# Extra unread matmuls in TensorE's waits, and another order of GpSimd's extra work, in a decoder layer on one core

## The reference

```python
x = layernorm(x + attention(x))              # 16 heads of 16, causal, softmax
x = layernorm(x + mamba(ctx, gate=x))        # state space block, see below
x = layernorm(x + moe(x))                    # 8 experts, the 2 best of each token
```

```python
state = state * exp(delta_t * A[n]) + (delta_t * u_t) * B_t[n]
y_t  += state * C_t[n]
y = (y + D * u) * silu(x)
```

## Time and profile before

| | us |
|---|---|
| median of 3 runs | 428.63 (428.04 to 429.7) |
| the profiled execution, its own time | 431.48 |
| its span in the trace | 429.7 |
| TensorE matmuls, busy | 340.4 (79%) |
| VectorE, busy | 252.1 (59%) |
| ScalarE, busy | 209.9 (49%) |
| GpSimd, busy | 248.5 (58%) |
| mean granted clock of TensorE | 0.878 |

### The profile page before, as it was taken

The page is one execution under the profiler, slowest core; times in us unless marked ns, Lnnn a source line. Parts: engine busy times, 40 slices in busy tenths (PEclk is TensorE's granted clock), DMA queues, the critical chain, the costliest instruction groups (busy, mean ns, idle before and its releaser), DMA issues.

```text
span 429.7 us, 5678 instructions
## 1 busy us (share of the span) xinstructions
PE 340.4 (79%) x1780; PEld 205.5 (48%) x1780; DVE 252.1 (59%) x439; ACT 209.9 (49%) x488; POOL 248.5 (58%) x232
## 2 busy tenths in 40 slices
PE   8794868856778677875869586899999999999651
PEld 4352435623446244653435242466666666666441
DVE  2989797974958879688977676112122222222134
ACT  4678786737877678767964100322222222212103
POOL 2075999999978996789888302233233333331214
PEclk9986596965989769896986888999999999999967
DMA  7050110162114510242106950111111111111162
GB/s 209 8 101 3 38 35 31 47 219 50 50 50 82 188 50 26 65 148 84 51 24 218 374 193 0 49 41 46 37 51 49 50 49 37 50 37 38 37 195 99
DMA packets 29455, 34.46 MB, mean 80 GB/s; under 512 B 4074, under 2 KB 23826, under 8 KB 29426
## 3 DMA queue, kind: packets, MB, share of 16 engines
q1 hardware_dynamic: 24770, 26.36, 20.3%
q0 software_dynamic: 2208, 6.03, 4.6%
q10 hardware_dynamic: 2448, 1.71, 1.4%
HBM read 28.92 MB, written 5.18 MB: 79 GB/s over the span
## 4 chain that ended last, share of the span: by engine, by line
PE 36%; DVE 6%; DMA 2%; ACT 2%; POOL 2%; issue 2%; DVEq 0%; POOLq 0%; ACTq 0%
PE psS L1600 18%; PE psD L1619 5%; PE psO L1619 4%; PE psD L1610 2%; PE psS L1450 2%; PE psT L1595 1%; DMA c_rows<-z_out 1%; DVE experts L981 1%; POOL rstd L493 1%; DVE u_sb L1131 1%; PE psT L1379 1%; DMA delta<-x_rows,row_in 1%; DMA z_out<-delta,row_out 1%; PE psT L1444 0%; POOL rstd L492 0%
## 5 line engine op out<-in xcount | busy, mean ns | idle before, releaser
L1600 PE MATMUL psS<-experts,delta 128*128 x184 | 86.5, 593 | 0.5 <-ACT delta L818 0.5
L504 POOL TENSOR_TENSOR experts<-experts,c_rows 128x1024 f32<-128x1024 f32 x31 | 73.0, 2355 | 17.8 <-DVE experts L981 17.4
L981 DVE TENSOR_TENSOR_SCAN experts<-experts,psD 128x512 f32<-128x512 f32 x64 | 74.4, 1204 | 0.0
L572 POOL DMA_INDIRECT z_out<-delta,row_out x23 | 22.8, 991 | 88.4 <-ACT delta L832 88.4
L1379 PE MATMUL psT<-ident,probs_at 128*128 128x128 f32 x192 | 39.2, 340 | 23.4 <-ACT probT L727 23.4
L1205 DVE COPY u_sb<-psD 128x512 f32<-128x512 f32 x23 | 15.9, 692 | 68.7 <-PE psD L1610 68.7
L689 ACT ACTIVATE experts<-delta,A_sb 128x255 f32<-128x255 f32 x128 | 54.7, 517 | 0.5 <-DVE du L929 0.5
L972 DVE TENSOR_TENSOR psD<-du,psD 128x512 f32<-128x512 f32 x64 | 41.6, 688 | 13.2 <-PE psD L1337 12.9
L1600 PEld LDWEIGHTS psS<-experts,delta 128*128 128x128 f32 x184 | 33.1, 190 | 24.3 <-issue 23.3
L1379 PEld LDWEIGHTS psT<-ident,probs_at 128*128 128x128 f32 x192 | 27.4, 172 | 35.1 <-ACT probT L727 33.4
L507 POOL TENSOR_TENSOR experts<-experts 128x512 f32<-128x512 f32 x31 | 40.7, 1312 | 2.4
(11 more groups left out here) (236 smaller groups left out, 591.6 us busy)
## 6 DMA issues: line engine op xcount, KB each, us to landing
c_rows<-c_dram SPq DMA_DIRECT2D x32, 256.0 KB, 3.4
experts<-in_L_ffn_w_gate_dram SPq DMA_DIRECT2D x8, 512.0 KB, 5.9
experts<-in_L_ffn_w_up_dram SPq DMA_DIRECT2D x8, 512.0 KB, 6.9
experts<-in_L_ffn_w_down_dram SPq DMA_DIRECT2D x8, 512.0 KB, 8.1
x_in<-in_x_dram SPq DMA_DIRECT2D x4, 256.0 KB, 5.3
x_rows<-x_sb SPq DMA_DIRECT2D x4, 256.0 KB, 2.5
probs_at<-z_out SPq DMA_DIRECT2D x4, 256.0 KB, 5.1
c_rows<-z_out ACTq DMA_DIRECT2D x4, 256.0 KB, 6.3
```

The source lines that it names most:

```text
L504: pool.tensor_tensor(states[:, g % ST], states[:, g % ST], c_rows[:, g % CR].rearrange("p n (o s) -> p n o s", o=1).broadcast_to([P, 2, HA ...
L981: dve.tensor_tensor_scan(states[:, g % ST, n].rearrange("p h s -> p (h s)"), dA[:, g % DA, n].rearrange("p h s -> p (h s)"), psD[:, n, :], ...
L1600: ins = pe.matmul(psS[:, bank, :], xgT[:, s % 2, k, :], gate_up_of(bass.ds(e, 1), i)[:, k, :], start=(k == 0), stop=(k == FC - 1))
```

## The change

GpSimd does both splits and all four fixes before its first product. The inverse deviation of batch b moves from ahead of the first product of batch b + 1 into the last product of batch b, behind its first instruction (for the last batch, whose last product is VectorE's, it stays). `keep_warm` takes a bank. TensorE gets unread matmuls: fourteen at step 0 of the first batch and eight at step 0 of the later ones (into `psT`), two, one and four at step 4 of each batch, two more there in the last one, and twenty-four in front of the combination. Two waits for `prob_rdy` that an earlier wait of the same engine includes are left out.

```diff
@@ -478,9 +478,10 @@
 
             pool.wait_ge(zeroed, 1 + DA)
             pool.wait_ge(ones_rdy, 1)
-            split_bc(0)
-            fix_log(0)
-            fix_log(1)
+            for th in range(TH):
+                split_bc(th)
+            for b in range(B):
+                fix_log(b)
 
             def inverse_deviation(k, n, done, count):
 
@@ -504,10 +505,12 @@
                 pool.tensor_tensor(states[:, g % ST], states[:, g % ST], c_rows[:, g % CR].rearrange(
                     "p n (o s) -> p n o s", o=1).broadcast_to([P, 2, HALVES, S]), ALU.mult).then_inc(hC_rdy, 1)
                 pool.wait_ge(hC_rdy, g + 1)
+                b, m = divmod(g, NP)
+                if m == NP - 1:
+                    inverse_deviation(2 * b, 0, x1_rdy, b)
                 pool.tensor_tensor(states[:, g % ST, 0], states[:, g % ST, 0], states[:, g % ST, 1],
                                    ALU.add).then_inc(pair_rdy, 1)
                 pool.wait_ge(pair_rdy, g + 1)
-                b, m = divmod(g, NP)
                 if m == 0:
                     pool.wait_ge(skip_rdy, HALVES * (b + 1))
                 else:
@@ -522,15 +525,8 @@
             link(pool.memset(exponent[:], -0.5))
             for b in range(B):
                 for m in range(NP):
-                    if m == 0 and b > 0:
-                        inverse_deviation(2 * (b - 1), 0, x1_rdy, b - 1)
                     if NP * b + m < STEPS - 1:
                         multiply_c(NP * b + m)
-                    if b == 0 and m < 2:
-                        fix_log(2 + m)
-                    elif b == 0 and m == 4:
-                        pool.wait_ge(y_sum, 5)
-                        split_bc(1)
                     if m == 1 and b > 0:
                         gate_output(b - 1)
                     if m == 3 and b > 0:
@@ -1445,9 +1441,9 @@
                                         start=(k == 0), stop=(k == FC - 1))
                 ins.then_inc(logit_ps, 1)
 
-            def keep_warm(n):
+            def keep_warm(n, bank=psS[:, 3, :]):
                 for _ in range(n):
-                    pe.matmul(psS[:, 3, :].rearrange("p (k n) -> p k n", n=P), ident_b[:],
+                    pe.matmul(bank.rearrange("p (k n) -> p k n", n=P), ident_b[:],
                               mask_qk[:].rearrange("p (o n) -> p o n", o=1).broadcast_to([P, BANK // P, P]),
                               start=True, stop=True)
 
@@ -1490,23 +1486,34 @@
                     more = b + 1 < B
                     if m < GROUPS:
                         scores(G)
+                    if g == 0:
+                        keep_warm(14, psT[:])
                     if m < GROUPS:
                         broadcast_b(g + 1, 0)
                         broadcast_b(g + 1, 1)
+                    if m == 0 and g > 0:
+                        take_turn(("prob", 3 * G))
+                        keep_warm(8, psT[:])
                     if 2 <= m <= 5:
                         turn_back(G - 2)
                     if 1 <= m <= 4:
                         transpose_probs(G - 1, 0)
                         if m == 4:
+                            keep_warm(2)
                             broadcast_b(g + 1, 0)
                         transpose_probs(G - 1, 1)
                         if m == 4:
                             broadcast_b(g + 1, 1)
                             if more:
-                                pe.wait_ge(prob_rdy, GROUPS * GH * (b + 1))
                                 transpose_x(b + 1)
+                            else:
+                                keep_warm(2)
                         transpose_probs(G - 1, 2)
+                        if m == 4:
+                            keep_warm(1)
                         weigh_values(G - 1)
+                        if m == 4:
+                            keep_warm(4)
                         if m == 2 and f >= 0:
                             transpose_gated(f)
                     elif m == 5:
@@ -1516,7 +1523,6 @@
                         if f >= 0:
                             transpose_x2(f)
                         if not more:
-                            pe.wait_ge(prob_rdy, GROUPS * GH * B)
                             keep_warm(6)
                         if more:
                             project_qk(b + 1, 0, 0, psS[:, 1, :], q_ps)
@@ -1658,6 +1664,7 @@
                                     stop=(i == TOPK - 1))
                 ins.then_inc(z_sum, 1)
 
+            keep_warm(24)
             pe.wait_ge(diag_rdy, TOPK * NT // QC)
             for t in range(NT // QC):
                 combine(t)
```

## The result

The changed kernel takes **423.35 us** (median of 4 runs, 420.17 to 425.25) against 428.61 (428.04 to 429.7, 4 runs): a ratio of 0.9856, 95% interval 0.9822 to 0.989. Its profiled execution took 423.88 (span 422.1) against 431.48 (span 429.7) before.

The account below looks back on a forecast made before the run. Bounds: TensorE's half-rate clock, the chain of waits, ScalarE's wait for `shift`, GpSimd's backlog. Terms 0.1 - 3.65 + 1.0 - 4.4 + 0 - 0.7 = -7.65 gave 423.8 profiled, 421.0 after carrying over 2.85; range 415 to 426.5.

Parts of the forecast that it names:

- three signs of being wrong: Unchanged VectorE wait for b=1's third scores; step 4 fillers at 0.43 us with longer broadcast wait; first fix late at 31.8.
- GpSimd's queue, -3.65: Step 1 of b=1: ScalarE's 4.29 us wait for `shift` goes, transposes then come last; -3.65 us.
- The du products, +1.0: VectorE's du products of b=1 and b=2 fall beside GpSimd's two-input work, the first hidden by a wait: +1.0 us.
- The first fix, +0.1: Before the first sums: GpSimd's first fix ends at 31.8, just where VectorE asks for it (31.80): +0.1 us.
- The clock in steps 0 to 2, -4.4: Unread matmuls hold TensorE's clock in each batch's first steps; two thirds of 6.6 taken: -4.4 us, bounds 0 and -6.6.
- Steps 4 and 5, 0: Unread matmuls around step 4's broadcast and weighing: 0 taken, between -4.2 (clock holds) and +8 (half rate) us.
- The combination, -0.7: Twenty-four unread matmuls in TensorE's 7.93 us idle: -1.4 if the clock holds, 0 if it falls; -0.7 us taken.
- Profile to median, 2.85: The profiled execution stood 2.85 us above the runs' median, 428.63; carried over from 423.8 to reach 421.0.
- A: Rival: the clock holds everywhere, -14.75 us, so 413.9; chance 0.12.
- B: Rival: the clock falls back in step 1 each time, gain is the queue's alone, -2.6 us: 426.0; chance 0.18.
- C: Rival: slower, step 4's unread matmuls run at half rate ahead of the broadcast, +8.0 us: 434.0; chance 0.05.
- D: Rival: the reorder doesn't free ScalarE, VectorE's maxima end the wait, the clock's gain is lost: 428.1; chance 0.05.

Follow-up runs that it names:

- reorder_only: Kernel before with GpSimd's part of the change alone (splits and fixes first, inverse deviation inside the last product), no new unread matmuls: 427.79 us, ratio 0.9957.
- warm_only: The changed kernel with GpSimd's old order, so all the unread matmuls and nothing else: 425.95 us, ratio 0.9922.
- first_only: Kernel before with both splits and all four fixes first, the inverse deviation where it was: 427.41 us, ratio 0.9962.
- idle_order: Kernel before with inverse deviation inside the eighth product and second split in GpSimd's idle time before its first product, no fillers: 424.09 us, ratio 0.9885.
- idle_no_step0: idle_warm without the fourteen and the eight unread matmuls of step 0: 423.95 us, ratio 0.9881.
- no_step4: The changed kernel without the unread matmuls of step 4: 423.85 us, ratio 0.9882.
- idle_warm: idle_order with all the unread matmuls of the change: 419.31 us, ratio 0.9754.
- change_again: The changed kernel itself, run once more beside the later runs: 422.92 us, ratio 0.9862.
- idle_step1: idle_warm with twenty instead of fourteen unread matmuls at first step 0, and five plus two in each batch's step 1: 418.29 us, ratio 0.9759.

## Why the prediction was right, and where it was not

The forecast was 421.0 in 415 to 426.5; 423.35 is inside, faster, and both parts of the mechanism named are borne out: the queue by reorder_only, the fillers by warm_only. The gain, 5.3 us, is less than the 7.6 forecast. Of what was to show it, four things came: no wait for `shift`, the wait of 2.36 down to 0.55, GpSimd's first product at 44.69 and inverse deviation at 86.02, and the 2.10 down to 0.83 (not in the second profile). Two didn't: the wait of 4.59 is 1.74, not under 1.5, and of the six slices named only the 15th has a clock of 9. Two of its three signs of being wrong came as well: the first fix was late, and a pair of fillers at step 4 took 0.53 us apiece while VectorE waited longer for the broadcast. The steps, against the two profiled executions:

- **GpSimd's queue, -3.65: right, and with it came more than was counted.** The wait for `shift` is gone. In first_only it is gone too, at nearly the clock of before (0.83 in b=1, before 0.81), and b=1 gave 3.6. In reorder_only and idle_order b=1 gave 5.0 and 4.9, at 0.90, without a filler, and VectorE's wait for the third scores was 1.68 in reorder_only against 3.55 in first_only. That the other 1.4 are the clock's is likely; why it was higher in those two is not shown.
- **The du products, +1.0 (bounds 0 to 3): the mis-sized term.** b=0 with the order alone is 3.1 longer, and VectorE is 4.7 us busier in it. I had priced one more contention at 1.64 - 0.69, from a du that met the add on 512 elements. The du of b=1 met the product on 1024 and took 2.72, and the sum ahead of it rose from 1.08 (the same place in idle_order) to 1.41. The wait that I let hide it, the 2.50 for scores, did shrink, but the delay is longer than that, and in reorder_only it falls on the du of b=2 and b=3 again. In the changed kernel's profile the last of them, at 62.51, came when GpSimd had no such work, took 0.69, and VectorE is 2.2 busier only.
- **The first fix, +0.1: 1.35 us of waiting**, 0.71 in first_only and 0.99 in reorder_only. I took the time at which VectorE asked, 31.80, from one execution; in the changed kernel's it asked at 30.01. GpSimd's first fix began at 26.84 there and ended at 31.32, about as forecast. What this cost is smaller than the wait: the du product behind it, at 32.48, took 0.69, where before, beside the second fix, the one at 32.52 took 1.76. With the 0.41 by which the sum at 31.36 is longer that makes some 0.7 us in all, and the 1.07 stand in no term of the prediction.

```profile
32.52 1.76 DVE L929 TENSOR_TENSOR du<-delta,u_sb 128x512 f32<-128x512 f32 x1
```

- **The clock in steps 0 to 2, -4.4.** It held in the second scores of b=2 (waits 1.09 and 0.55), fell in b=0 at step 1 (0.50 from 40 to 52 us), ahead of step 0's fillers in b=1, and once more in b=3, where the wait for the third scores rose from 0.59 to 1.76. What is left after the queue's 5.0 and the loss in b=0 is 0.9 - 3.1 = -2.2 in b=0, -0.1 in b=1, -1.1 in b=2 and -1.3 in b=3: together -4.7, step 4 included. That it is so near to the -4.4 is no proof of that term. In b=0 a part is the last du, which met nothing, and single batches vary by as much. Not all of it is the fillers' either: reorder_only, without any, is 0.5 and 1.0 shorter in b=2 and b=3 as well. That step 0's fillers are needed for it, idle_no_step0 bears out, in the other order.
- **Steps 4 and 5, 0 (from -4.2 to +8).** In the change's first profile the pair ahead of the broadcast ran at half rate and made VectorE's wait 1.60 instead of 0.74 in b=0, b=1 and b=2, as the prediction feared; in b=3 it is 0.55. Little of these 0.86 is lost: the next wait is shorter, in b=1 0.38 (at 118.03) instead of the 1.15 at 123.59. For the change itself no_step4 is the test, and by it the sum is a gain of 0.2 to 0.3%, about 1 us, that can't be told from the 0 forecast. In idle_warm's order it is 0.8%, nearer to the lower end.
- **The combination, -0.7.** The wait went from 2.10 to 0.83 and 0.70, so -0.6 in this execution, but 2.09 stayed in change_again. A steady gain of 0.7 is not shown.
- **Profile to median, 2.85.** The terms add up to -7.65 and the two profiled executions differ by 431.48 - 423.88 = 7.60. The medians differ by 5.3, since the changed kernel's profiled execution is only 0.5 above its median and not 2.85: this step accounts for the 2.35 by which the forecast was too low. The agreement of the terms is partly luck: the queue's larger gain and the larger loss in b=0 cancel, and the first scan began 1.1 earlier although the first fix was late.

The rivals: A falls, the clock still falls in each batch (the windows). B falls with warm_only and idle_no_step0, where the fillers do gain, though the clock did fall back in step 1 of b=0, as B has it. C's price is seen (1.06 us for two, a wait 0.86 longer), but the next wait takes most of it back, and no_step4 shows no loss. D falls with reorder_only's b=1.

The Trainium skill's rule on shared ports ("GPSIMD Engine Reference", "8. Key points") is borne out, and costs more here than I read it: see below. The Trainium skill's rule that transposes don't engage the full clock ("TensorE: Matmul & The Clock Gate", "Part 4: PE-mode transpose") made the clock of rival A unlikely. In b=2 of idle_step1 the clock is 1.00 through the whole batch, and the sets of four transposes of probabilities ran in 0.60 to 0.66 us there. The prediction took the 0.66 at 161.15 as weak support of that rule; it rather speaks against it. So they run at the full clock when it is granted; whether they would hold it by themselves is not shown, since scores, the weighing of values and, at steps 0, 1 and 4, unread matmuls stand among them.

**Still open:** why the clock falls at one filler group in one execution and not in another; what the twenty-four are worth; why step 4's fillers gain more in one order than in the other; whether idle_step1 is better than idle_warm.

## What to carry to other kernels

Extra work of an engine is best put into the idle time that engine already has: here, with the split in GpSimd's 4.47 us gap and two fixes left in place, the new order gained 1.15%, with split and fixes ahead of all 0.43%. When work is moved, look up what the neighbour engine will be running at the new time, not only who waits for it. And where unread matmuls are used, judge by many runs: their effect on the clock is not the same in each.

## What was not expected of the hardware

**A VectorE operation of 128 x 512 with two SBUF inputs that starts during GpSimd's two-input instruction ends some 0.55 us after that one ends.** By the rows it is held rather than slowed. In the fourteen profiles this is so for each sum and du product that starts in such an instruction: 0.54 to 0.56, without an exception. In the change GpSimd's product runs from 44.69 for 2.64, to 47.33, and the du of 45.16 ends at 47.88; GpSimd's add ends at 54.09 + 1.59 = 55.68, the du at 56.24. In first_only the same, with a du of 2.87. VectorE first, then GpSimd:

```profile
64.41 2.87 DVE L925 TENSOR_TENSOR du<-delta,u_sb 128x512 f32<-128x512 f32 x1
```

```profile
64.38 2.34 POOL L505 TENSOR_TENSOR experts<-experts,c_rows 128x1024 f32<-128x1024 f32 x1
```

The du starts 0.03 after GpSimd's product and ends at 67.28, 0.56 after its end at 66.72. GpSimd's instruction is itself longer where it starts while such a VectorE operation runs: 2.64 instead of 2.35 at 44.69, during the sum of 43.71, and 1.59 instead of 1.27 at 54.09. The product of first_only, which started first, was not (2.34). So a 0.69 us operation costs anything up to 2.9, by when it starts. Beside GpSimd's one-input instruction the du took 0.69 (45.95), but a sum that began 0.07 us after such an instruction did, at 44.83 before, took 1.08, against 0.68 at 31.80; so that isn't always free either. In the earlier trace rows the 1.64 at 62.62 is the same: it ends at 64.26, and GpSimd's add (1.60) at 63.72.

**The same program's clock differs between executions.** The changed kernel's four had mean clocks from 0.918 to 0.950 and times from 425.25 to 420.17. The two at 0.918 are 1.4 us apart, so the clock isn't all of that spread. Set-up, which ended between 36.1 and 37.8 us in the traced executions with this order, may be another part.
